# GQA in a Trainium2 decoder kernel: the queries' squares summed by TensorE in fp32, without the split into two bf16 parts

## The chip, the cores and the metric

The kernel runs on one core of one Trainium2 chip. The metric is the device time of one execution in microseconds (us), as the median of several runs.

## The reference, cut to what matters

A two-layer decoder on 64 sequences of 64 tokens with 256 features. Its first block is a grouped-query attention: 16 query heads and 4 key heads of 128 features, each head normalised by its own mean and variance (the layer norm of the queries is the part that the change touches), rotary embedding, causal softmax, output projection. Five more blocks follow (a cross attention, a feed-forward with low-rank experts, a multi-query attention, a second cross attention, a quantised feed-forward), which the change leaves alone.

```python
    def _layernorm(x, g, b):
        mu = jnp.mean(x, axis=-1, keepdims=True)
        var = jnp.mean(jnp.square(x - mu), axis=-1, keepdims=True)
        return (x - mu) * jax.lax.rsqrt(var + EPS) * g + b
    ...
    qkv = jnp.einsum('bsh,oh->bso', x, w_qkv)
    ...
    q = _layernorm(q, qn_g, qn_b)
    k = _layernorm(k, kn_g, kn_b)
    ...
    scores = jnp.einsum('bhqd,bhkd->bhqk', q, k) / jnp.sqrt(jnp.float32(D))
```

## The kernel before

The tokens are 32 tiles of 128 (two sequences each), kept in SBUF for the whole program. Each block of the decoder is a stage of its own that runs over the 32 tiles; the stages follow one another. Within a stage every engine has its own program, in order, and semaphores join them. `over_tiles` writes out the first two and the last two tiles and loops over the rest, two tiles per turn.

In the GQA stage (`attention_gqa`, with the helpers of the class `Attend`) the work of two or three neighbouring tiles is interleaved by hand: in the step of tile t, each engine does the scores and the softmax of t, the projections, squares and rotation of the queries and keys of t + 1, and the values and the output projection of t - 1. The weights are centred per head beforehand, so a head's variance is the mean of the squares of its projected features. Features lie along the partitions and (head, token) along the columns, so a sum over features is a matmul with ones.

The queries of a tile are made in four groups of four heads, one PSUM bank each (`queries`, L103 to L105 through `mm3`). For each group g:

- ScalarE squares the bank into `sq` in fp32 (L596), squares it again into `sqh` in bf16 (L597), and copies the two halves of the features swapped into `qsw` (L600).
- GpSimd multiplies `qsw` by a table into `w` (`swapped_part`, L540), then takes `sql = sq - sqh` as bf16 (`squares_low`, L545).
- VectorE multiplies the bank by another table into `u` (`rotate_query`, L679) and adds `w` (`add_swapped`, L684).

TensorE's order in a step is: transposes of the probabilities of t - 1 (L387), transposes of the normalised x (L274), the scores' bias (L803), the scores (L822), the query sums (`query_sums`, L811 and L812), keys (`mm3` with `a_wk`), values, key sums (L774, fp32, one matmul per key head with `m.ones[:, 0:1]` moving), the first group of queries, the turned scores (L829), values by probabilities (L408), and then the three other groups of queries and the output projection in two halves. The scores wait for all four `add_swapped` (`uw_ready`) and for ScalarE's copy of the transposed probabilities (L393, `pt_ready`), because both use PSUM banks 4 and 5.

On VectorE, the query sums are taken out by L710 into `vq`; GpSimd raises it to the power -1/2 into `rq` (L558); VectorE scales the turned scores by it (L716), adds bias and mask (L720), takes the low part of the first half of the attention output (`ol`, L427; its high part `oh` is ScalarE's L422), the maximum (L355), and so on; L443 adds the output projection to x. GpSimd also subtracts the maximum (L359), scales the probabilities (L379), and takes the layer norm's power (L254, L256) for which VectorE's L266 waits.

Of the kernel before, what the change touches and what calls it, by code (L numbers as in the profile page):

```python
# [20 lines left out]
BF16 = mybir.dt.bfloat16  # L21
ACT = mybir.ActivationFunctionType
AX = mybir.AxisListType.X

P = 128
TILES = 32
SEQ = 64
# [20 lines left out]
def wait_used(eng, sem, t, buffers, per_tile=1, last=0):  # L48

    if isinstance(t, int) and t < buffers:
        return
    eng.wait_ge(sem, (t - buffers) * per_tile + (last or per_tile))
# [158 lines left out]
def spread(a, n):  # L212

    return a.rearrange("p (k o) -> p k o", o=1).to_broadcast([a.shape[0], a.shape[1], n])

def repeat(a, n):

    return a.rearrange("p (o k) -> p o k", o=1).to_broadcast([a.shape[0], n, a.shape[1]])
# [78 lines left out]
HEADS, HD = 16, 128  # L298
# [152 lines left out]
def attention_gqa(m):  # L451
# [9 lines left out]
    with ExitStack() as ctx:  # L461
        sb = lambda n, s, t=F32: ctx.enter_context(nc.sbuf_tensor("a0_" + n, s, t))
        sem = ctx.enter_context(Semaphores(nc, "a0_"))
        ps = ctx.enter_context(nc.psum_tensor("a0_ps", [P, 8, 512], F32))
# [17 lines left out]
        w = sb("w", [P, 2, HEADS, SEQ])  # L482
        qsw = sb("qsw", [P, 2, HEADS, SEQ])
        sq = sb("sq", [P, 2, HEADS, SEQ])
        sqh = sb("sqh", [P, 2, HEADS, SEQ], BF16)
        sql = sb("sql", [P, 2, HEADS, SEQ], BF16)
        st = sb("st", [P, HEADS, SEQ])
        sqk = sb("sqk", [P, NK])
        kt = sb("kt", [P, NK])
# [9 lines left out]
        chain, pool_chain = sem("chain"), sem("pool_chain")  # L499
        k_ready, vp_ready, q_ready, ksum_ready = (sem(n) for n in ("k_ready", "vp_ready", "q_ready", "ksum_ready"))  # L500
        ksw_ready, qsw_ready, u_ready, w_ready = (sem(n) for n in ("ksw_ready", "qsw_ready", "u_ready", "w_ready"))
        sqh_ready, sql_ready, stp_ready, st_ready = sem("sqh_ready"), sem("sql_ready"), sem("stp_ready"), sem("st_ready")
        sqk_ready, sq_ready, uw_ready = sem("sqk_ready"), sem("sq_ready"), sem("uw_ready")
        kraw_ready, vk_ready, rkd_ready, rkb_ready, kt_ready = (sem(n) for n in ("kraw_ready", "vk_ready", "rkd_ready", "rkb_ready", "kt_ready"))
        s2_ready, var_ready, vq_ready, rq_ready = sem("s2_ready"), sem("var_ready"), sem("vq_ready"), sem("rq_ready")
        at_.v_ready = sem("v_ready")
        further = lambda t: not (isinstance(t, int) and t + 2 >= TILES)
        QBANK = (2, 1, 0, 3)
        s2_ps = ps[:, 6, :]
        sct = at_.sc  # L510
        var_ps = ps[:, 7, 0:HEADS]
        heads_of = lambda a: a.rearrange("p (h b s) -> p h b s", h=4, b=2)
        pair_of = lambda a, k, b: a[:, b, 2 * k:2 * k + 2, :].rearrange("p h s -> p (h s)")
        by_head = lambda a, g: a[:, :, 4 * g:4 * g + 4, :].rearrange("p b h s -> p h b s")
# [12 lines left out]
        @block.gpsimd  # L527
        def _(pool):
            def key_rstd(t):
                pool.wait_ge(vk_ready, t + 1)  # L530
                pool.tensor_tensor(rk[:, :], vk[:, :], m.mhalf[:, 0:KV], ALU.pow).then_inc(pool_chain, 1)
                pool.wait_ge(pool_chain, t + 1)
                wait_used(pool, rkb_ready, t, 1)
                pool.tensor_tensor(rkd[:, :, :], repeat(m.ident[:, :], KV), spread(rk[:, :], P), ALU.mult).then_inc(rkd_ready, 1)

            def swapped_part(t, g):

                pool.wait_ge(qsw_ready, 4 * t + g + 1)
                wait_used(pool, uw_ready, t, 1, 4, g + 1)
                pool.tensor_tensor(by_head(w, g), by_head(qsw, g), table(QW), ALU.mult).then_inc(w_ready, 1)  # L540

            def squares_low(t, g):
                pool.wait_ge(sqh_ready, 4 * t + g + 1)
                wait_used(pool, var_ready, t, 1)
                pool.tensor_tensor(by_head(sql, g), by_head(sq, g), by_head(sqh, g), ALU.subtract).then_inc(sql_ready, 1)  # L545

            def head():
                ln.pool(pool)
                ln.pool_step(pool, 1, 1)
                key_rstd(0)  # L550
                pool.wait_ge(tab_set, 1)
                for g in range(4):
                    swapped_part(0, g)
                    squares_low(0, g)

            def step(t, p, has_next):
                pool.wait_ge(vq_ready, t + 1)
                pool.tensor_tensor(rq[:, :], vq[:, :], m.mhalf[:, 0:HEADS], ALU.pow).then_inc(rq_ready, 1)  # L558
                if has_next:
                    key_rstd(t + 1)  # L560
                    swapped_part(t + 1, 0)
                    squares_low(t + 1, 0)
                at_.subtract_max(pool, t)
                if has_next:
                    swapped_part(t + 1, 1)
                    squares_low(t + 1, 1)
                at_.normalise(pool, t)
                if further(t):
                    ln.pool_step(pool, t + 2, p)
                if has_next:  # L570
                    for g in (2, 3):
                        swapped_part(t + 1, g)
                        squares_low(t + 1, g)
            over_tiles(pool, head, step)

        @block.scalar
        def _(act):
            def square_keys(t):
                act.wait_ge(k_ready, t + 1)
                wait_used(act, ksum_ready, t, 1)  # L580
                act.activation(sqk[:, :], ps[:, 1, :], ACT.Square).then_inc(sqk_ready, 1)
                wait_used(act, kraw_ready, t, 1)
                for to, of in swapped:
                    last = act.copy(ksw[to, :], ps[of, 1, :])
                last.then_inc(ksw_ready, 1)

            def value(t, p):
                act.wait_ge(vp_ready, t + 1)
                wait_used(act, at_.pv_ready, t, 2, 2)
                act.activation(at_.v[:, p, :], ps[:, 3, :], ACT.Copy, scale=1.0 / WS).then_inc(at_.v_ready, 1)  # L590

            def square(t, g):
                act.wait_ge(q_ready, 4 * t + g + 1)
                wait_used(act, var_ready, t, 1)
                wait_used(act, sql_ready, t, 1, 4, g + 1)
                act.activation(by_head(sq, g), heads_of(ps[:, QBANK[g], :]), ACT.Square).then_inc(sq_ready, 1)  # L596
                act.activation(by_head(sqh, g), heads_of(ps[:, QBANK[g], :]), ACT.Square).then_inc(sqh_ready, 1)  # L597
                wait_used(act, w_ready, t, 1, 4, g + 1)
                for to, of in swapped:
                    last = act.copy(by_head(qsw[to], g), heads_of(ps[of, QBANK[g], :]))  # L600
                last.then_inc(qsw_ready, 1)

            def scores_out(t):
                act.wait_ge(stp_ready, t + 1)
                wait_used(act, at_.sc_ready, t, 1)
                act.copy(st[:, :, :], sct).then_inc(st_ready, 1)

            def head():
                ln.high(act, 0, 0, q_ready, 4)
                square_keys(0)  # L610
                value(0, 0)
                for g in range(4):
                    square(0, g)

            def step(t, p, has_next):
                before = not (isinstance(t, int) and t == 0)
                if before:
                    at_.copy_transposed(act, t - 1)
                if has_next:
                    ln.high(act, t + 1, 1 - p, q_ready, 4)  # L620
                scores_out(t)
                if has_next:
                    square_keys(t + 1)
                    square(t + 1, 0)
                if before:
                    at_.high(act, t - 1, 0)
                if has_next:
                    square(t + 1, 1)
                at_.exponential(act, t)
                if has_next:  # L630
                    value(t + 1, 1 - p)
                if before:
                    at_.high(act, t - 1, 1)
                if has_next:
                    square(t + 1, 2)
                    square(t + 1, 3)
            over_tiles(act, head, step)
            at_.copy_transposed(act, TILES - 1)
            at_.high(act, TILES - 1, 0)
            at_.high(act, TILES - 1, 1)  # L640
# [111 lines left out]
        def _(pe):  # L752
# [51 lines left out]

            def query_sums(t):

                pe.wait_ge(sql_ready, 4 * (t + 1))
                for b in range(2):
                    for k in range(PAIRS):
                        out = var_ps[:, 2 * k + b:2 * k + b + 1]  # L810
                        pe.matmul(out, pair_of(sqh, k, b), m.onesb[:, :], start=True, stop=False)  # L811
                        last = pe.matmul(out, pair_of(sql, k, b), m.onesb[:, :], start=False, stop=True)  # L812
                last.then_inc(var_ready, 1)

            def scores(t):
# [58 lines left out]
            t, p = TILES - 1, 1  # L874
# [1761 lines left out]
```

## Time and profile before

| | |
|---|---|
| median of 3 runs | 3523.93 us (3517.58 to 3548.65) |
| profiled execution | 3515.81 us, with a span of 3514.0 us from the first to the last instruction |
| mean granted TensorE clock | 0.886 of 2.4 GHz |
| busy: TensorE, VectorE, GpSimd, ScalarE | 2828.3, 2080.2, 1604.8, 1574.2 us |
| scores of the first and of the last GQA tile start at | 86.7 us and 971.6 us |

A profile row gives a start (or a count), a duration, the engine, the line of the kernel, the tensors and their shapes; in brackets stands how long the engine had been idle before it and which instruction released it. PE is TensorE's matmul, DVE is VectorE, ACT is ScalarE, POOL is GpSimd. A matmul's recorded duration includes its way through the array, so neighbouring matmuls overlap in the records; how long a group occupies the engine is read from the start of its first record to the start of the next group. A fp32 matmul shows as two records.

### The profile page before, as it was taken

Reading aid. Unit: us, or ns where it says so; the run is one execution under the profiler, and the core shown is the slowest. Engines: PE = TensorE matmul, PEld = TensorE weight load, DVE = VectorE, ACT = ScalarE, POOL = GpSimd, SP = SyncE. Lnnn points to the kernel's source line nnn. Section 1 sums busy time; section 2 is a strip of 40 time slices with the busy share of each in tenths; the row PEclk is TensorE's granted clock in tenths of the full one; section 3 lists DMA queues with packets and bytes.
Section 4 is the critical chain, followed back from the end, with each engine's and each line's share of the span. In section 5 each row is a group of like instructions: output and inputs, shape, how many; then the busy total and the mean of one; then the engine's idle time right before and its main releaser. Section 6 shows DMA issues by size and latency. Waiting matters only on the chain. (4 is left out here: it accounts for less than half of the span.)

```text
span 3514.0 us, 84894 instructions
## 1 busy us (share of the span) xinstructions
PE 2828.3 (80%) x32044; PEld 2042.3 (58%) x32044; DVE 2080.2 (59%) x3785; ACT 1574.2 (45%) x2718; POOL 1604.8 (46%) x1643
## 2 busy tenths in 40 slices
PE   1788888888857887776699996999999999995665
PEld 1666666666622222223477775878878878884332
DVE  4677777777747667756566663444444444443786
ACT  2555555555516556661233332333333333331665
POOL 1777777777722222213222213545545545541332
PEclk9899999999967557788888888999999999997666
DMA  3000000000012222210000000000000000000000
GB/s 110 1 0 0 0 0 0 0 0 0 0 45 74 69 70 73 79 47 9 19 21 24 21 21 11 7 6 7 7 5 7 7 5 7 7 2 26 12 18 18
DMA packets 94065, 73.24 MB, mean 21 GB/s; under 512 B 17314, under 2 KB 88354, under 8 KB 93218
## 3 DMA queue, kind: packets, MB, share of 16 engines
q1 hardware_dynamic: 93860, 70.14, 6.6%
q8 instruction: 174, 2.85, 0.3%
q14 instruction: 31, 0.25, 0.0%
HBM read 51.76 MB, written 17.04 MB: 20 GB/s over the span
## 5 line engine op out<-in xcount | busy, mean ns | idle before, releaser
L1294 DVE TENSOR_REDUCE x_mx<-x_ps 128x2 f16<-128x512 f32 x512 | 329.8, 682 | 102.1 <-PE x_ps L1356 99.2
L1263 ACT ACTIVATE x_e<-x_ps 128x512 f32<-128x512 f32 x512 | 285.0, 595 | 73.5 <-PE x_ps L1360 67.8
L1356 PE MATMUL x_ps<-x_k,x_q 32*128 32x256 f16 x1024 | 199.1, 336 | 128.2 <-ACT x_e L1263 56.5
L1628 ACT ACTIVATE x_sq<-x_ps 128x512 f32<-128x512 f32 x256 | 152.1, 595 | 310.0 <-PE x_ps L1767 303.2
L1356 PEld LDWEIGHTS x_ps<-x_k,x_q 32*128 32x128 f16 x1024 | 52.9, 97 | 291.2 <-DVE x_mx L1294 153.6
L540 POOL TENSOR_TENSOR a_w<-a_qsw,a_tab 128x512 f32<-128x512 f32 x128 | 218.4, 1706 | 7.9 <-ACT a_qsw L600 6.6
L103 PE MATMUL x_ps<-x_chi,x_w 128*128 128x128 f16 x1024 | 200.3, 221 | 14.3 <-ACT x_rkb L1649 7.5
L1360 PE MATMUL x_ps<-x_q,x_k 32*128 32x256 f16 x1024 | 200.1, 338 | 3.0 <-ACT x_e L1263 2.8
L103 PE MATMUL x_ps<-ln_xhx,x_w 128*128 128x128 f16 x1024 | 198.2, 219 | 1.7 <-DVE x_k L1687 1.7
L104 PE MATMUL x_ps<-x_clo,x_w 128*128 128x128 f16 x1024 | 199.5, 220 | 0.0
L105 PE MATMUL x_ps<-x_chi,x_w 128*128 128x128 f16 x1024 | 199.4, 220 | 0.0
L104 PE MATMUL x_ps<-ln_xlx,x_w 128*128 128x128 f16 x1024 | 197.9, 219 | 0.0
L105 PE MATMUL x_ps<-ln_xhx,x_w 128*128 128x128 f16 x1024 | 197.9, 219 | 0.0
L103 PE MATMUL a_ps<-a_wo,a0oh 128*128 128x256 f16 x512 | 142.8, 279 | 66.2 <-DVE a0ol L427 66.2
L1393 PE MATMUL x_ps<-x_e,x_vt 128*9 128x256 f32 x2048 | 192.4, 510 | 0.9 <-ACT x_e L1263 0.9
L1576 POOL TENSOR_TENSOR x_sum<-x_sum,x_sq 128x512 f32<-128x512 f32 x128 | 162.4, 1268 | 63.1 <-ACT x_sq L1628 57.7
L359 POOL TENSOR_TENSOR x1s<-x1s,x1mx 128x1024 f32<-128x1024 f32 x32 | 60.8, 1901 | 283.1 <-DVE x1mx L355 283.1
L103 PE MATMUL a_ps<-ln_xha,a_wq 128*128 128x128 f16 x1024 | 179.9, 221 | 8.7 <-DVE a_kt L673 8.7
L427 DVE TENSOR_TENSOR x1ol<-x_ps,x1oh 128x1024 f16<-128x1024 f32 x64 | 78.4, 1225 | 180.6 <-ACT x1oh L422 180.6
L104 PE MATMUL a_ps<-ln_xla,a_wq 128*128 128x128 f16 x1024 | 179.3, 221 | 0.0
L105 PE MATMUL a_ps<-ln_xha,a_wq 128*128 128x128 f16 x1024 | 179.3, 221 | 0.0
L545 POOL TENSOR_TENSOR a_sql<-a_sq,a_sqh 128x512 bf16<-128x512 f32 x128 | 164.1, 1282 | 0.0
(343 smaller groups left out, 9699.8 us busy)
## 6 DMA issues: line engine op xcount, KB each, us to landing
x_q<-x_q_rows SPq DMA_DIRECT2D x32, 256.0 KB, 2.7
x_k<-x_k_rows SPq DMA_DIRECT2D x32, 256.0 KB, 3.1
a_stage<-in_x_w SPq DMA_DIRECT2D x32, 256.0 KB, 2.6
x_vt<-in_ctx_v SPq DMA_DIRECT2D x32, 144.0 KB, 2.3
x_all<-in_x SPq DMA_DIRECT2D x8, 512.0 KB, 7.8
x_cf<-in_ctx SPq DMA_DIRECT2D x32, 128.0 KB, 2.1
x_q_rows<-x_xhl SPq DMA_DIRECT2D x32, 128.0 KB, 1.8
x_k_rows<-x_chl SPq DMA_DIRECT2D x32, 128.0 KB, 1.8
```

The source lines that it names most:

```text
L103: pe.matmul(out, a[0], b[0], start=start, stop=False)
L104: pe.matmul(out, a[0], b[1], start=False, stop=False)
L105: return pe.matmul(out, a[1], b[0], start=False, stop=stop)
L540: pool.tensor_tensor(by_head(w, g), by_head(qsw, g), table(QW), ALU.mult).then_inc(w_ready, 1)
L545: pool.tensor_tensor(by_head(sql, g), by_head(sq, g), by_head(sqh, g), ALU.subtract).then_inc(sql_ready, 1)
L1263: act.activation(e[:, u % ES].rearrange("p c n -> p (c n)"), s2_ps(u), ACT.Exp, scale=XT ** -0.5).then_inc(e_ready, 1)
L1294: dve.reduce_max(mx[:, p % 2, c:c + 2], s1_ps(u), AX).then_inc(mx_ready, 1)
L1356: return pe.matmul(s1_ps(u)[:, c], q[r, p % 4, g, c * P:(c + 1) * P], k[r, p % 4, g], start=True, stop=True)
L1360: return pe.matmul(s2_ps(u)[:, c * DM:(c + 1) * DM], k[r, p % 4, g, c * P:(c + 1) * P], q[r, p % 4, g], start=True, stop=True)
L1393: last = pe.matmul(o_ps[32 * jj:32 * jj + VC, g % 2, :], vt[:, p % 2, n, u, :], e[:, u % ES, n, :], start=n == 0, stop=n == KC - 1)
L1576: pool.tensor_tensor(sum4[:, :], sq[:, 0, :] if g == 1 else sum4[:, :], sq[:, g, :], ALU.add).then_inc(sum4_ready, 1)
L1628: act.activation(sq[:, e % 4, :], ps[:, bank(e), :], ACT.Square).then_inc(act_left, 1)
```

## The change

ScalarE no longer writes `sqh`, and GpSimd no longer writes `sql`; both tensors and their semaphores are gone. TensorE sums `sq` directly in fp32, with the 128 columns of a pair of heads as weights and a column of ones moving: 16 matmuls per tile with fp32 operands in the place of 32 with bf16 operands. It waits for `sq_ready` in the place of `sql_ready`.

```diff
@@ gpsimd
-            def squares_low(t, g):
-                pool.wait_ge(sqh_ready, 4 * t + g + 1)
-                wait_used(pool, var_ready, t, 1)
-                pool.tensor_tensor(by_head(sql, g), by_head(sq, g), by_head(sqh, g), ALU.subtract).then_inc(sql_ready, 1)
...
-                    squares_low(0, g)
...
-                    squares_low(t + 1, 0)
...
-                    squares_low(t + 1, 1)
...
-                        squares_low(t + 1, g)
@@ scalar, square(t, g)
-                wait_used(act, sql_ready, t, 1, 4, g + 1)
                 act.activation(by_head(sq, g), heads_of(ps[:, QBANK[g], :]), ACT.Square).then_inc(sq_ready, 1)
-                act.activation(by_head(sqh, g), heads_of(ps[:, QBANK[g], :]), ACT.Square).then_inc(sqh_ready, 1)
@@ tensor, query_sums(t)
-                pe.wait_ge(sql_ready, 4 * (t + 1))
+                pe.wait_ge(sq_ready, 4 * (t + 1))
                 for b in range(2):
                     for k in range(PAIRS):
-                        out = var_ps[:, 2 * k + b:2 * k + b + 1]
-                        pe.matmul(out, pair_of(sqh, k, b), m.onesb[:, :], start=True, stop=False)
-                        last = pe.matmul(out, pair_of(sql, k, b), m.onesb[:, :], start=False, stop=True)
+                        last = pe.matmul(var_ps[:, 2 * k + b:2 * k + b + 1], pair_of(sq, k, b), m.ones[:, 0:1], start=True, stop=True)
```

## Rows read from the trace of the kernel before

**Rows 1.** The page: busy time by engine, and the group of L545.

```profile
PE 2828.3 (80%) x32044; PEld 2042.3 (58%) x32044; DVE 2080.2 (59%) x3785; ACT 1574.2 (45%) x2718; POOL 1604.8 (46%) x1643
...
L545 POOL TENSOR_TENSOR a_sql<-a_sq,a_sqh 128x512 bf16<-128x512 f32 x128 | 164.1, 1282 | 0.0
```

**Rows 2.** Windows: length, busy PE, PEld, DVE, ACT, POOL, granted clock, DMA.

```profile
400.00:500.00 100.00, 82.55 (x946) 64.12 (x943) 70.70 (x100) 54.86 (x87) 76.11 (x52) 1.00 0.00 0
```

**Rows 3.** Timeline of VectorE: L716 of the third and the 31st tile.

```profile
158.93 1.23 DVE L716 TENSOR_TENSOR a0s<-a_ps,a_rq 128x1024 f32<-128x1024 f32 x1 [0.54 <-PE a_ps L829]
...
952.90 1.23 DVE L716 TENSOR_TENSOR a0s<-a_ps,a_rq 128x1024 f32<-128x1024 f32 x1 [0.54 <-PE a_ps L829]
```

**Rows 4.** Waits in the GQA stage: us in total, times, longest.

```profile
DVE a_u L684 <- POOL a_w L540: 38.3, 31, 1.2
```

**Rows 5.** Timeline of VectorE in one tile.

```profile
501.86 1.22 DVE L427 TENSOR_TENSOR a0ol<-a_ps,a0oh 128x1024 f16<-128x1024 f32 x1
...
513.20 1.35 DVE L266 TENSOR_SCALAR ln_xna<-x_all,ln_mva,ln_rstda 128x256 f32 x1 [0.45 <-POOL ln_rstda L256]
...
515.07 0.41 DVE L443 SCALAR_TENSOR_TENSOR x_all<-a_ps,x_all 128x256 f32 x1
515.40 0.71 DVE L684 TENSOR_TENSOR a_u<-a_u,a_w 128x512 f32<-128x512 f32 x1
517.34 1.56 DVE L684 TENSOR_TENSOR a_u<-a_u,a_w 128x512 f32<-128x512 f32 x1 [1.23 <-POOL a_w L540]
...
527.57 1.23 DVE L716 TENSOR_TENSOR a0s<-a_ps,a_rq 128x1024 f32<-128x1024 f32 x1 [0.54 <-PE a_ps L829]
```

**Rows 6.** Timeline of GpSimd in the same tile.

```profile
512.06 1.11 POOL L256 TENSOR_TENSOR ln_rstda<-ln_vea,mhalf 128x1 f32<-128x1 f32 x1
513.14 1.26 POOL L540 TENSOR_TENSOR a_w<-a_qsw,a_tab 128x512 f32<-128x512 f32 x1
514.36 1.20 POOL L545 TENSOR_TENSOR a_sql<-a_sq,a_sqh 128x512 bf16<-128x512 f32 x1
515.52 1.72 POOL L540 TENSOR_TENSOR a_w<-a_qsw,a_tab 128x512 f32<-128x512 f32 x1
517.19 1.16 POOL L545 TENSOR_TENSOR a_sql<-a_sq,a_sqh 128x512 bf16<-128x512 f32 x1
522.15 2.90 POOL L558 TENSOR_TENSOR a_rq<-a_vq,mhalf 128x16 f32<-128x16 f32 x1 [3.80 <-DVE a_vq L710]
```

**Rows 7.** Timeline of ScalarE in the same tile.

```profile
500.65 1.01 ACT L422 CAST a0oh<-a_ps 128x1024 f16<-128x1024 f32 x1
...
502.22 0.59 ACT L597 ACTIVATE a_sqh<-a_ps 128x512 bf16<-128x512 f32 x1
...
516.73 1.01 ACT L393 COPY a0pt<-a_ps 128x1024 f32<-128x1024 f32 x1 [3.57 <-PE a_ps L387]
```

**Rows 8.** Timeline of TensorE in the same tile.

```profile
515.63 1.06 PE L387 MATMUL a_ps<-ident,a0e 128*128 128x128 f32 x8 [1.85 <-DVE x_all L443]
...
516.75 1.02 PE L803 MATMUL a_ps<-a_kt,a_bq 128*128 128x512 f32 x2
518.95 1.95 PE L822 MATMUL a_ps<-a_u,a_kt 128*64 128x256 f32 x16 [1.18 <-DVE a_u L684]
520.83 0.18 PE L811 MATMUL a_ps<-onesb,a_sqh 128*128 128x1 bf16 x1
...
521.65 0.22 PE L103 MATMUL a_ps<-ln_xha,a_wk 128*128 128x128 f16 x1
...
524.28 0.95 PE L774 MATMUL a_ps<-ones,a_sqk 128*128 128x1 f32 x8
525.09 0.22 PE L103 MATMUL a_ps<-ln_xha,a_wq 128*128 128x128 f16 x1
```

**Rows 9.** Timelines of VectorE and TensorE before the first scores.

```profile
82.57 4.05 DVE L684 TENSOR_TENSOR a_u<-a_u,a_w 128x512 f32<-128x512 f32 x4
...
86.67 3.68 PE L822 MATMUL a_ps<-a_u,a_kt 128*64 128x256 f32 x16 [4.96 <-DVE a_u L684]
```

More of the change, by code:

```diff
@@ L484, in attention_gqa @@
         sq = sb("sq", [P, 2, HEADS, SEQ])
-        sqh = sb("sqh", [P, 2, HEADS, SEQ], BF16)
-        sql = sb("sql", [P, 2, HEADS, SEQ], BF16)
         st = sb("st", [P, HEADS, SEQ])
@@ L501, in attention_gqa @@
         ksw_ready, qsw_ready, u_ready, w_ready = (sem(n) for n in ("ksw_ready", "qsw_ready", "u_ready", "w_ready"))
-        sqh_ready, sql_ready, stp_ready, st_ready = sem("sqh_ready"), sem("sql_ready"), sem("stp_ready"), sem("st_ready")
+        stp_ready, st_ready = sem("stp_ready"), sem("st_ready")
         sqk_ready, sq_ready, uw_ready = sem("sqk_ready"), sem("sq_ready"), sem("uw_ready")
```

## The prediction

> **What bounds the kernel now.** The page comes first [rows 1]: the change touches only the first attention (GQA, to about 1,004 us), and TensorE is the busiest engine of the whole. The page's chain that ended last is no help: it covers only the final instructions of the last stage. So the stage is read on its own. In a stretch of 100 us there TensorE shows 82.6 us busy, GpSimd 76.1, VectorE 70.7, ScalarE 54.9, at a granted clock of 1.00, the 2.4 GHz level [rows 2]. No engine is full: the tile is bound by a loop that passes through several of them. L716, the scaling of the scores, starts once per tile, and its first and last regular starts, 158.93 and 952.90, are 28 tiles apart: 28.36 us per tile [rows 3], with the same wait each time. One tile can therefore stand for all.
>
> I follow the loop backwards from L716 at 527.57. It waits for TensorE (0.54 us, the turned scores) [rows 5]. TensorE has had no gap since the scores' matmuls at 518.95: scores, query sums, keys, values, key sums, first queries, turned scores all follow in program order [rows 8]. The scores waited for the last addition of the rotated queries, L684, that ends at 517.34 + 1.56 = 518.90 [rows 5]. This in turn waited for GpSimd's product L540, which ends at 515.52 + 1.72 = 517.24 [rows 6]; the list of waits has this one in 31 tiles, 38.3 us in all [rows 4]. Ahead of it VectorE is in one nearly unbroken row from L716 to the residual L443, which ends at 515.48 and lets TensorE start its transposes at 515.63 [rows 5, 8]. So a tile is: VectorE's long stretch, then the join of L684 with GpSimd's L540, then TensorE's unbroken stretch of 8.6 us from the scores to the next L716.
>
> **TensorE's part: on the path.** Old: 32 matmuls with bf16 weights of 128 columns and one moving column occupy TensorE from 520.83 to 521.65, 0.82 us [rows 8]. New: 16 with fp32 weights. The kernel already has this very form, in the key sums L774: four matmuls, which the trace shows as eight records, from 524.28 to the next operation at 525.09, so 0.81 us, or 0.20 per matmul [rows 8]. Sixteen make 3.24 us, so the step grows by 2.42 us. The first load hides under the matmul ahead in both places. A run of 32 records need not go exactly like one of eight, and the key sums' end is read off the next operation's start. Bounds for the 16: 3.0 and 3.5 us, growth 2.2 to 2.7.
>
> The row first: a fp32 load-and-multiply record follows the last one after 0.10 us, a bf16 one after 0.026 [rows 8]. The Trainium skill (TensorE: Matmul & The Clock Gate, "Weight-path perf modes" and "LDWEIGHTS") says that the fast weight load is off for fp32 weights and that an ordinary load takes the number of columns over 1.2 ns, 107 ns for 128 columns. This rule speaks against the change; an estimate by that page is 32 times 0.107, or 3.41 us, 0.17 us a tile or 5 us in all more than by the row.
>
> Behind these matmuls on TensorE's queue wait the keys, the values, the key sums, the first queries and the turned scores, and L716 waits for the last of them. There is no wait in this stretch that could absorb the 2.42. GpSimd's power L558 (for the queries' factors) shifts by as much: it begins at 522.15 and ends at 525.06, 2.5 us ahead of L716 [rows 5, 6], and as both shift alike it stays ahead.
>
> **GpSimd's part: L545 goes.** Four subtractions per tile, 1.28 us each in the mean [rows 1], 5.1 us. Most of this buys nothing. Behind L540 of groups 0 and 1 GpSimd waits for VectorE's maximum or denominator anyway, and those two L545 are in that idle time. What counts is the L545 of group 2, between the two last products [rows 6], and that of group 3. The rows show GpSimd and VectorE taking turns: L684 with both inputs in SBUF takes 0.68 to 0.71 alone, but the last one takes 1.56 and ends 0.55 after GpSimd's L545 (517.19 + 1.16 = 518.35; 518.90). L540 takes 1.26 alone and 1.72 where L684 runs before it [rows 5, 6]. The Trainium skill (SBUF — State Buffer, on the shared port pair) calls this an exclusive lock, held for the whole instruction, against GpSimd for VectorE's operations with two SBUF inputs; this trace agrees.
>
> New order, in the times of the old tile, with 0.12 us taken off throughout: the cast L422 at 500.65 waits for ScalarE's copies, which come one L597 (0.59) earlier; its product is wanted at 501.86, and L427 can start only when VectorE's preceding addition ends, which I put at 501.74 [rows 5, 7]. The power L256, L540 of group 2 (513.02 to 514.28) and L266 (to 514.43) keep their order. L540 of group 3 comes next, and with the port free from 514.43 takes 1.13: to 515.56. L684 of group 2 waits for it and ends 0.55 later, 516.11. L684 of group 3 follows directly, with nothing of GpSimd's in the way, and ends at about 516.8. The join moves from 518.90 to 516.8: 2.1 us.
>
> **What is late next.** TensorE cannot use all of it. Its transposes L387 wait for L443 (now 515.36), so they start at 515.51; the bias matmul L803 starts at 516.63 and its records end at 517.65. And the scores overwrite the banks that L393, ScalarE's copy of the transposed probabilities, reads: L393 begins when L387 is through and ends at 516.73 + 1.01 - 0.12 = 517.62 [rows 7, 8]. Scores then start at 517.68 and not at 518.95: 1.27 us gained per tile. Bounds: 0.9, if L803's queue or the semaphores take 0.35 more; 1.6, if the 0.12 turns out as 0.4.
>
> **ScalarE's part: L597 goes.** Four of 0.59 us [rows 7]. ScalarE waits for TensorE before the squares and idles after the last copies, so this is worth only the 0.12 above. No DMA, and no queue of SP's, is touched. The wait of the sums is now on ScalarE's square and not on GpSimd's remainder; both are long done at 520.8, so this is worth nothing; if that cover were gone it would cost the distance from the square to the sums.
>
> **The sum.** Per regular tile 2.42 - 1.27 = +1.15 us. All 32 tiles pay the 2.42: +77.4. Tiles 1 to 31 take back 1.27: -39.4. The start: before the first scores ScalarE does four L597, two of them ahead of the keys for which the third group of queries waits, and GpSimd's L545 stretch the four additions L684 to 4.05 us [rows 9] instead of four steps of 0.6 plus one wait; I work out 2.1 us earlier for ScalarE's last copy and 1.0 for the additions, -3.1. In tile 1 the limit by L393 is absent (its probabilities are early), so about 1.4 more comes back there. The two first score blocks run at a clock near 1.2 GHz (3.68 us against 1.95 [rows 8, 9]); the fp32 sums behind them would be dearer by up to 3 us each, and some of that comes back because the clock rises in the same stretch while later work benefits: +1 net, bounds -2 to +5. Together 77.4 - 39.4 - 3.1 - 1.4 + 1 = +34.5 us.
>
> The profiled execution took 3515.8 us around a span of 3514.0; with the sum it would be 3550. The runs of before have a median of 3523.9, lowest 3517.6: the profile is at their lower end, 8 us under the median. Against the median I forecast 3558. About 1% is what a measurement of this kernel can tell from no change, and the sum is 0.98% of the median: whether it is called slower or the same is nearly a toss.
>
> **The rivals.**
> (1) No recovery. Another wait takes the place of L540's, and the scores start no earlier. For it: VectorE's rows are dense, and L803 and L393 are only 1.2 us behind. Against it: both rows show their ends, and neither waits for the removed work. All of the 2.42 is then paid: 77.4 - 3.1, so +74, 3598 us.
> (2) Cheaper sums. Long runs of fp32 loads with one column pipeline better than four; the sixteen take 2.4 us (0.075 per record). For it: the four L774 stand between other forms. Against it: eight equal records are already a run. The growth is 1.6, the tile +0.3, the total about 32 x 0.82 = 26 less: +8, 3532 us.
> (3) The port turns the other way: this is the faster case. L256 and L684 of group 1 come to the port within 0.05 us, L256 takes 1.11 and loses about 0.55; L266 comes 0.06 after L540 of group 2 and takes 1.35, some 0.9 of it waiting [rows 5, 6]. The 0.12 shift, or GpSimd's emptier queue, could let L256 and L266 go first. Then L443, TensorE's transposes and the scores are up to 1.45 us earlier, the tile goes to 2.42 - 1.27 - 1.45 = -0.30, and the total to -10: 3514 us. It turns to a gain from 1.15 us on. Against it: all four operations hang on the same denominator and shift together, so that the order should stay. That alone is under 1%; with cheaper sums, or a larger gain before the scores, it would pass 1%.
>
> **How the numbers follow.** Forecast with its bounds 0.67, rival 1 0.10, rival 2 0.12, rival 3 0.11. The forecast's own bounds: growth less gain from 2.2 - 1.6 = 0.6 to 2.7 - 0.9 = 1.8 us a tile, so +18 to +55 us; against 3517 to 3524 as the base 3535 to 3579. The range reaches over half of rival 2 and part way to rival 1: 3532 to 3585. Slower by over 1%: half of the forecast less a little (its sum is just under 1%), 0.34, and rival 1, 0.10: 0.44. Faster by over 1%: 0.06, the part of rival 3 that comes together with cheaper sums. The same: 0.50, the rest of all of them.
>
> **What the next profile would show.** Right: L716 regularly 29.5 us apart; the sums from the first record to the keys' first matmul 3.2 us; L684 of the last group 0.68 and no longer 1.56; scores waiting for ScalarE's copy L393 or following L803 at once; GpSimd idle 5 us more per tile. Wrong: a distance of 30.8 (rival 1), sums of 2.4 (rival 2), L266 at about 0.45 (rival 3). What would upset all of it is a granted clock other than 1.00 in the regular tiles, where I count on no change because TensorE's share of busy time rises.

## The result and the profile after

The changed kernel takes 3707.9 us (median of 4 runs, 3694.5 to 3720.3) against 3521.9 for the kernel before (median of 4 runs now): 1.051 times as long, with an interval of 1.047 to 1.055. The forecast was 3558 us with 3585 as its upper end. The kernel is slower by 186 us where 35 were forecast.

The page after, busy times and granted clock:

```profile
PE 3038.8 (82%) x32044; PEld 2220.8 (60%) x32044; DVE 2081.2 (56%) x3785; ACT 1512.9 (41%) x2590; POOL 1405.2 (38%) x1515
...
PEclk9988898898887578765878887999999999998566
```

GpSimd lost 200 us of work and ScalarE 61, and TensorE gained 210 [rows 1 for before]. As far as the 13th slice, where the first attention ends, the clock's digits are now mostly 8, where the tiles of before ran at 1.00 [rows 2]. The lines have new numbers: L703 is the scaling of the scores (was L716), L707 adds bias and mask (L720), L671 is the addition of the rotated queries (L684), L538 GpSimd's product (L540), L797 the query sums (L811, L812), L807 the scores (L822), L761 the key sums (L774).

VectorE's timeline, with the first and the last regular start of L703 and one tile between:

```profile
160.60 1.23 DVE L703 TENSOR_TENSOR a0s<-a_ps,a_rq 128x1024 f32<-128x1024 f32 x1 [1.54 <-PE a_ps L814]
...
502.22 1.22 DVE L703 TENSOR_TENSOR a0s<-a_ps,a_rq 128x1024 f32<-128x1024 f32 x1 [1.54 <-PE a_ps L814]
503.48 2.12 DVE L707 TENSOR_TENSOR a0s<-a0s,a_s2m 128x1024 f32<-128x1024 f32 x1
505.74 1.23 DVE L427 TENSOR_TENSOR a0ol<-a_ps,a0oh 128x1024 f16<-128x1024 f32 x1
...
518.94 0.41 DVE L443 SCALAR_TENSOR_TENSOR x_all<-a_ps,x_all 128x256 f32 x1
519.27 1.42 DVE L671 TENSOR_TENSOR a_u<-a_u,a_w 128x512 f32<-128x512 f32 x2
...
536.42 1.23 DVE L703 TENSOR_TENSOR a0s<-a_ps,a_rq 128x1024 f32<-128x1024 f32 x1 [1.52 <-PE a_ps L814]
...
1116.64 1.23 DVE L703 TENSOR_TENSOR a0s<-a_ps,a_rq 128x1024 f32<-128x1024 f32 x1 [1.54 <-PE a_ps L814]
```

A tile takes (1116.64 - 160.60) / 28 = 34.14 us, 5.79 more than before [rows 3]. GpSimd's and ScalarE's rows of the same tile:

```profile
501.63 1.04 POOL L532 TENSOR_TENSOR a_rkd<-ident,a_rk 128x512 f32<-128x512 f32 x1
503.24 1.27 POOL L538 TENSOR_TENSOR a_w<-a_qsw,a_tab 128x512 f32<-128x512 f32 x1 [0.57 <-ACT a_qsw L587]
```

```profile
520.59 1.01 ACT L393 COPY a0pt<-a_ps 128x1024 f32<-128x1024 f32 x1 [4.53 <-PE a_ps L387]
```

TensorE's timeline, in two stretches of the same tile:

```profile
521.75 1.95 PE L807 MATMUL a_ps<-a_u,a_kt 128*64 128x256 f32 x16
523.62 4.81 PE L797 MATMUL a_ps<-ones,a_sq 128*128 128x1 f32 x32
528.29 0.27 PE L103 MATMUL a_ps<-ln_xha,a_wk 128*128 128x128 f16 x1
...
530.81 0.63 PE L103 MATMUL a_ps<-a_wv,ln_xha 128*128 128x512 f16 x1
...
533.13 0.95 PE L761 MATMUL a_ps<-ones,a_sqk 128*128 128x1 f32 x8
```

And windows (length, busy PE, PEld, DVE, ACT, POOL, granted clock, DMA) over that stretch:

```profile
522.00:525.00 3.00, 3.00 (x29) 2.40 (x25) 0.93 (x2) 1.01 (x1) 0.00 (x0) 1.00 0.00 0
525.00:526.00 1.00, 1.00 (x12) 1.00 (x11) 0.00 (x0) 0.00 (x0) 0.00 (x0) 1.00 0.00 0
526.00:527.00 1.00, 1.00 (x7) 1.00 (x7) 0.00 (x0) 0.00 (x0) 0.00 (x0) 0.52 0.00 0
527.00:532.00 5.00, 5.00 (x34) 4.26 (x35) 0.17 (x1) 0.92 (x2) 2.90 (x1) 0.50 0.00 0
532.00:533.00 1.00, 1.00 (x4) 0.39 (x3) 0.12 (x1) 0.83 (x2) 0.00 (x0) 0.56 0.00 0
533.00:534.00 1.00, 1.00 (x12) 0.97 (x11) 1.00 (x2) 0.00 (x0) 0.00 (x0) 1.00 0.00 0
```

These are the rows to look at.
The tile of before (499.19 to 527.57, [rows 5, 8]) and this one (502.22 to 536.42), piece by piece along the loop of the prediction. Of the tile of before these rows are wanted as well, from VectorE and GpSimd:

```profile
499.19 1.23 DVE L716 TENSOR_TENSOR a0s<-a_ps,a_rq 128x1024 f32<-128x1024 f32 x1 [0.54 <-PE a_ps L829]
500.45 1.27 DVE L720 TENSOR_TENSOR a0s<-a0s,a_s2m 128x1024 f32<-128x1024 f32 x1
```

```profile
499.60 1.04 POOL L534 TENSOR_TENSOR a_rkd<-ident,a_rk 128x512 f32<-128x512 f32 x1
500.79 2.06 POOL L540 TENSOR_TENSOR a_w<-a_qsw,a_tab 128x512 f32<-128x512 f32 x1
```

| piece, us | before | after | difference |
|---|---|---|---|
| L716/L703 to the end of the residual L443 | 16.29 | 17.13 | +0.84 |
| to the first score matmul | 3.47 | 2.40 | -1.07 |
| scores | 1.88 | 1.87 | 0 |
| query sums, to the first key matmul | 0.82 | 4.67 | +3.85 |
| keys and values, to the key sums | 2.63 | 4.84 | +2.21 |
| to the next L716/L703 | 3.29 | 3.29 | 0 |

The last L703 of the stage starts 165.9 us later than L716 did (1144.1 against 978.2), and that is the change's doing. The other 29 us between the two profiled executions (3710.5 and 3515.8) lie in later stages, whose code is the same. The second stage takes 521 us from its first to its last reduction before and 538 after, but between 494 and 552 in the kernels below, which leave it alone too. I did not look into what moves it; it also widens the intervals, so the tile's length in the trace is the sharper measure here.

### The profile page after: what moved, and what is told of

Read it like the earlier page. It is cut to its first block and busy times, and to the rows that moved or that the text cites. A ratio compares the mean times of both kernels' runs of the same rounds, so it can differ in the third digit from the quotient of the medians.

```text
span 3708.1 us, 84512 instructions
## 1 busy us (share of the span) xinstructions
PE 3038.8 (82%) x32044; PEld 2220.8 (60%) x32044; DVE 2081.2 (56%) x3785; ACT 1512.9 (41%) x2590; POOL 1405.2 (38%) x1515
## 5 line engine op out<-in xcount | busy, mean ns | idle before, releaser
L1378 PE MATMUL x_ps<-x_e,x_vt 128*9 128x256 f32 x2048 | 202.2, 532 | 0.9 <-ACT x_e L1248 0.9
L550 POOL TENSOR_TENSOR a_rq<-a_vq,mhalf 128x16 f32<-128x16 f32 x32 | 93.2, 2911 | 289.4 <-DVE a_vq L697 289.4
L538 POOL TENSOR_TENSOR a_w<-a_qsw,a_tab 128x512 f32<-128x512 f32 x128 | 177.9, 1399 | 21.1 <-ACT a_qsw L587 21.0
```

The costliest lines, as they stand in the source:

```text
L1378: last = pe.matmul(o_ps[32 * jj:32 * jj + VC, g % 2, :], vt[:, p % 2, n, u, :], e[:, u % ES, n, :], start=n == 0, stop=n == KC - 1)
```

## The experiments

The tile's length is the distance of the third from the 31st L716 (or its line in that kernel) over 28. The clock is that of the window from 200 to 800 us.

| run | what | ratio to before (interval) | median us | tile us | clock |
|---|---|---|---|---|---|
| before | | | 3521.9 | 28.36 | 1.00 |
| changed | | 1.051 (1.047 to 1.055) | 3707.9 | 34.14 | 0.90 |
| pe_only | fp32 sums, split kept | 1.048 (1.038 to 1.057) | 3688.9 | 33.51 | 0.93 |
| split_only | split gone, bf16 sums | 0.989 (0.982 to 0.997) | 3482.3 | 27.21 | 1.00 |
| wide_sums | 128 moving columns | 1.017 (1.009 to 1.024) | 3580.8 | 30.13 | 1.00 |
| bf16_long | 4 times the bf16 sums | 1.027 (1.019 to 1.035) | 3617.3 | 31.01 | 0.99 |
| fp16_squares | one fp16 square | 0.985 (0.982 to 0.989) | 3472.9 | 26.88 | 1.00 |
| port_wait | GpSimd waits for L703 | 1.035 (1.030 to 1.039) | 3650.9 | 32.55 | 0.92 |
| halves | 8 sums, keys, 8 sums | 1.022 (1.016 to 1.028) | 3595.9 | 30.85 | 1.00 |
| cols32 | 32 moving columns | 1.038 (1.034 to 1.041) | 3658.7 | 31.93 | 0.95 |
| halves_port | both of these | 1.012 (1.005 to 1.020) | 3579.0 | 30.00 | 1.00 |
| bf16_longer | 8 times the bf16 sums | one run | 3786.6 | 36.32 | 0.89 |

**Each part by itself.** First, which part brings the clock down.

```diff
 # before.py, query_sums; squares and split stay
-                        out = var_ps[:, 2 * k + b:2 * k + b + 1]
-                        pe.matmul(out, pair_of(sqh, k, b), m.onesb[:, :], start=True, stop=False)
-                        last = pe.matmul(out, pair_of(sql, k, b), m.onesb[:, :], start=False, stop=True)
+                        last = pe.matmul(var_ps[:, 2 * k + b:2 * k + b + 1], pair_of(sq, k, b), m.ones[:, 0:1], start=True, stop=True)
```

> TensorE's part alone: 16 fp32 matmuls with one moving column sum sq, while ScalarE's second square and GpSimd's subtraction stay, their results unused. Theory A, thin sums: a few us of matmuls with one moving column let the granted clock fall, in whatever type. Then the sums take about 4.7 us, keys and values run at half clock, and the tile is 28.4 + 3.9 + 2.2 = 34.5 us: about 3715 us. Theory B, fp32 itself: the same. Theory C, the rhythm: the clock falls because the removed work on ScalarE and GpSimd changed the waits of TensorE. Then the clock stays at 1.00 here, the tile is 28.4 + 2.4 = 30.8 us, and the time about 3600 us.

3688.9 us. The clock falls though ScalarE and GpSimd do all that they did before, so the rhythm of their work is not the cause (theory C). In 19 of the 28 tiles the whole price is there (33.9 to 34.4 us), in four part of it (32.8), and five take the 31.1 us of a full clock; why the clock spares these, where it falls in every tile of the changed kernel, stays open. In one of the five the sixteen sums take 3.60 us, from 464.77 to the first key matmul at 468.37. The tile at 575 us, in windows:

```profile
597.00:600.00 3.00, 3.00 (x29) 3.00 (x27) 0.00 (x0) 1.01 (x1) 0.00 (x0) 0.97 0.00 0
600.00:606.00 6.00, 6.00 (x37) 4.62 (x38) 0.34 (x2) 1.76 (x3) 2.90 (x1) 0.50 0.00 0
```

```diff
 # after.py: one square, in bf16; 32 sums of it
-        sq = sb("sq", [P, 2, HEADS, SEQ])
+        sq = sb("sq", [P, 2, HEADS, SEQ], BF16)
...
-                        last = pe.matmul(var_ps[:, 2 * k + b:2 * k + b + 1], pair_of(sq, k, b), m.ones[:, 0:1], start=True, stop=True)
+                        out = var_ps[:, 2 * k + b:2 * k + b + 1]
+                        pe.matmul(out, pair_of(sq, k, b), m.onesb[:, :], start=True, stop=False)
+                        last = pe.matmul(out, pair_of(sq, k, b), m.onesb[:, :], start=False, stop=True)
```

This kernel leaves the low part of the squares out and counts the high part twice, so its results are of no use; it is there for its time.

> The split's removal alone: ScalarE squares once, into bf16, GpSimd does nothing, and TensorE sums the same bf16 squares in 32 matmuls of one column, each tile twice, as many as before and in the same type (the sums are twice the squares' high parts). Theories A and B: clock 1.00 in every regular tile, sums 0.8 us, the scores 1.1 to 1.3 us nearer to the residual's end; tile 27.1 to 27.3 us and 3480 to 3490 us, unless GpSimd's first product takes the port ahead of VectorE's addition of bias and mask (L720), as in the changed kernel: then 0.85 us more per tile and 3510 us. Theory C: the clock falls in each tile here, and the time is above 3550 us.

3482.3 us, tile 27.21. The removal of the split is a gain, of the size expected: the scores start 2.40 us behind the residual's end (3.47 before). In 5 of the 28 tiles it is 26.8 and not 27.3; there the residual ends 0.5 us earlier. In each of them GpSimd's L256 takes 0.55 us and not 1.10, so it had the port ahead of VectorE's L671, which is half of rival 3; single tiles of other kernels do the same. No tile showed the other half, L266 ahead of GpSimd's product: L266 takes 1.3 us or more in all of them.

**Thin, or fp32.**

```diff
 # after.py, query_sums
-                for b in range(2):
-                    for k in range(PAIRS):
-                        last = pe.matmul(var_ps[:, 2 * k + b:2 * k + b + 1], pair_of(sq, k, b), m.ones[:, 0:1], start=True, stop=True)
+                for k in range(PAIRS):
+                    for b in range(2):
+                        i = 2 * k + b
+                        last = pe.matmul(ps[:, 7, i:i + P], pair_of(sq, k, b), m.ones[:, :], start=True, stop=True)
```

> The changed kernel, with 128 moving columns of ones in the place of one, in ascending order, so that each matmul's first column stays and the others are overwritten. The array is busy for nearly the same time (a fp32 record of 128 columns follows the last after 0.11 us, one of a single column after 0.10). Theory A: the clock stays at 1.00, sums 3.6 us, tile 28.4 + 2.8 - 1.1 + (0 to 0.85) = 30.1 to 31 us, 3570 to 3600 us, faster than the changed kernel though TensorE does more. Theory B: the clock falls as in the changed kernel or more, at least 3710 us.

3580.8 us and a tile of 30.13, 4.0 us less than with a single column, although TensorE streams 128 times the columns. Its window over the regular tiles, against that of the changed kernel:

```profile
200.00:800.00 600.00, 526.85 (x5349) 427.89 (x5347) 399.63 (x577) 286.73 (x437) 334.43 (x220) 1.00 0.00 0
```

```profile
200.00:800.00 600.00, 519.69 (x4714) 418.81 (x4712) 369.40 (x514) 253.61 (x386) 278.20 (x194) 0.90 0.00 0
```

The busy shares shown are 88% and 87%, the clocks 1.00 and 0.90: the two kernels cannot be told apart by the busy share. The type alone (theory B) is not the cause either, since the operands are fp32 in both. What differs is the number of moving columns, and the order of the sixteen (k before b); cols32 below has this same order, and there the clock falls, so the order is not what keeps it up.

```diff
 # before.py, query_sums: around both loops, 8 in bf16_longer
+                for _ in range(4):
...
```

> The kernel before with its bf16 sums done four times over: 128 matmuls of one column, about 3.3 us, as long as the fp32 sums should have been. Theory A: the clock falls here too, in about the same place; the sums themselves hardly notice (0.026 to 0.027 us each at either clock), keys and values take 2.2 us more: tile 28.4 + 2.4 + 2.2 = 33 us, about 3670 us. Theory B: the clock stays at 1.00, tile 30.8, about 3600 us.

> The kernel before with its bf16 sums done eight times over, 256 matmuls of one column, about 6.5 us. With four times over the clock fell in a few tiles only. If a thin stretch in bf16 counts as a lull like one in fp32, only less so, then at this length the clock falls in every tile, keys and values take 4.8 instead of 2.6 us, and the tile is 28.36 + 5.6 + 2.2 = 36.2 us, 3760 us. If only fp32 does it, the clock stays at 1.00, the tile is 34.0 us, and the time 3700 us.

Four times over, theory A was wrong as I had put it: the clock stays up in nearly all tiles (30.76 us each; 5 of the 28 took 32.2 to 32.4), the mean tile is 31.01, and not 33. Eight times over it falls in every tile: none of the 28 took the 34.0 us of a full clock, they took 35.4 to 37.6, mean 36.32, where I expected 36.2. So one-column matmuls in bf16 bring the clock down too: 3.2 us of them in few tiles, 6.7 us in every one. Whether bf16 needs a longer stretch than fp32 is not shown, since the fp32 sums take 3.6 us and no bf16 run has that length.

```diff
 # after.py, order k, b and i = 2 * k + b as in wide_sums
...
+                        last = pe.matmul(ps[:, 7, i:i + 32], pair_of(sq, k, b), m.ones[:, 0:32], start=True, stop=True)
```

> The changed kernel with 32 moving columns per fp32 sum instead of 1 or 128. Theory: what counts is how many columns stream per us. The sums should take 3.2 us, as their duration is set by the weight loads; if 32 columns are enough, the clock stays at 1.00 and the tile is 28.36 + 2.42 - 1.07 = 29.7 us, 0.4 less than with 128 columns; about 3565 us. If they are not enough, it falls as with one column: 34 us, about 3700.

Neither: tiles of 30.0 stand beside tiles of 34.2, with a mean of 31.93, and the clock is 0.95. The tiles of 30.0 are the changed kernel's tile at a full clock (the sums take 3.6 us there). What exactly brings the clock down stays open: with 32 columns per 0.11 us it fell in many tiles, and with one bf16 column per 0.026 us, over a slightly shorter stretch, in few.

**The length of the stretch.**

```diff
 # after.py: query_sums(t, b) does the 8 sums of sequence b
...
-                query_sums(t)
+                query_sums(t, 0)
                 if has_next:
                     keys(t + 1, 1 - p)
+                query_sums(t, 1)
+                if has_next:
                     value(t + 1, 1 - p)
```

> The changed kernel with 8 of the 16 fp32 sums ahead of the keys and 8 behind them. TensorE's work is the same, but a thin stretch is half as long. Theory: the length of the stretch brings the clock down; so it stays at 1.00 here, the tile is 28.36 + 2.42 - 1.07 = 29.7 us, and the time 3560 us or so. Rival: only the amount of thin work in a tile counts, however it is laid out; then the clock falls as in the changed kernel, and the time is about 3700 us.

The clock stays at 1.00 with exactly the same 16 thin fp32 matmuls; so it is not their amount per tile but the stretch in one piece. TensorE's timeline:

```profile
525.38 1.95 PE L796 MATMUL a_ps<-ones,a_sq 128*128 128x1 f32 x16
527.18 0.22 PE L103 MATMUL a_ps<-ln_xha,a_wk 128*128 128x128 f16 x1
...
528.52 1.90 PE L796 MATMUL a_ps<-ones,a_sq 128*128 128x1 f32 x16
```

The tile is 30.85 and not 29.7. The rows give both reasons. Eight sums take 1.80 us (525.38 to 527.18), so 16 take 3.6 and not 3.24. And the residual ends 17.12 us behind L703, not 16.3: the order at the port, which is turned here as in the changed kernel.

**The order at the port.**

```diff
 # after.py, GpSimd's step
                     key_rstd(t + 1)
+                    pool.wait_ge(at_.sc_left, t + 1)
                     swapped_part(t + 1, 0)
```

> The changed kernel, with GpSimd's first product of a tile (L538) waiting until VectorE has scaled the scores (L703), so that VectorE's L707 comes to the shared port first, as it did before. If the order at the port costs 0.85 us per tile, L707 goes from 2.1 to 1.27 us, the residual's end comes 16.3 us behind L703 instead of 17.1, and the tile from 34.14 to 33.3: about 26 us less than the changed kernel. If something else sets L427 and what follows, nothing changes. The clock still falls in each tile.

In the tile at 556 us, L707 (here L708) takes 1.23 again and the residual ends 16.24 us behind L703. Tiles with the whole low stretch take 33.3 (34.2 before the wait), as expected. In about every second tile the low stretch is shorter too (31.7 us), so the mean tile is 1.59 us shorter, 45 us over the 28. The run as a whole gained 57 us and not 26; the rest lies outside these tiles.

> The two halves of the sums, and GpSimd's wait of the run before last. If the clock and the order at the port are the only two things that went otherwise than forecast, then with both held off the changed kernel does what the forecast said, but for the sums' price, which the runs with a full clock put at 3.6 us and not 3.24: tile 28.36 + 2.75 - 1.07 = 30.0 us, clock 1.00, L707 1.23 to 1.27 us, the residual's end 16.3 us behind L703; about 53 us more than the kernel before, 3575 us. A third cause would leave it at 30.5 or more.

A tile of 30.00 us, in all 28 (29.98 to 30.02), as expected. GpSimd's and VectorE's rows:

```profile
526.12 1.04 POOL L532 TENSOR_TENSOR a_rkd<-ident,a_rk 128x512 f32<-128x512 f32 x1
527.71 2.14 POOL L538 TENSOR_TENSOR a_w<-a_qsw,a_tab 128x512 f32<-128x512 f32 x1 [0.54 <-DVE a0s L704]
```

```profile
526.23 1.22 DVE L704 TENSOR_TENSOR a0s<-a_ps,a_rq 128x1024 f32<-128x1024 f32 x1 [1.54 <-PE a_ps L815]
527.49 1.23 DVE L708 TENSOR_TENSOR a0s<-a0s,a_s2m 128x1024 f32<-128x1024 f32 x1
```

VectorE's L708 starts 0.22 us ahead of GpSimd's L538, and now it is L538 that is stretched. With clock and order both held off, the tile is what the forecast's terms give with the sums at their measured price: nothing else is left to explain in it. The median is 3579, where the forecast was 3558 and this run's own expectation 3575.

**A version that beats both.**

```diff
 # after.py
-        sq = sb("sq", [P, 2, HEADS, SEQ])
+        sq = sb("sq", [P, 2, HEADS, SEQ], F16)
...
-                act.activation(by_head(sq, g), heads_of(ps[:, QBANK[g], :]), ACT.Square).then_inc(sq_ready, 1)
+                act.activation(by_head(sq, g), heads_of(ps[:, QBANK[g], :]), ACT.Square, scale=1.0 / WS).then_inc(sq_ready, 1)
...
-                dve.tensor_scalar(vq[:, :], var_ps, 1.0, HD * LN_EPS * WS * WS, ALU.mult, ALU.add).then_inc(vq_ready, 1)
+                dve.tensor_scalar(vq[:, :], var_ps, WS * WS, HD * LN_EPS * WS * WS, ALU.mult, ALU.add).then_inc(vq_ready, 1)
...
-                        last = pe.matmul(var_ps[:, 2 * k + b:2 * k + b + 1], pair_of(sq, k, b), m.ones[:, 0:1], start=True, stop=True)
+                        last = pe.matmul(var_ps[:, 2 * k + b:2 * k + b + 1], pair_of(sq, k, b), m.onesh[:, 0:1], start=True, stop=True)
```

> ScalarE writes each square once, divided by 64 squared so that it fits, in fp16; TensorE sums it in 16 matmuls of one column with fp16 weights, and VectorE's L697 multiplies by 64 squared again. No split, no fp32 matmul. Theory thin and slow sums (a long stretch of one-column fp32 matmuls brings the clock down): the sums take 16 times 0.026, 0.4 us, clock 1.00, the scores 2.4 us behind the residual's end instead of 3.5; tile 28.36 - 0.41 - 1.07 = 26.9 us, 46 us less than the kernel before, about 3475 us. Theory C, the rhythm: the clock falls in this kernel as well.

3472.9 us, 0.985 of before (0.982 to 0.989), tile 26.88. The sums:

```profile
489.22 1.95 PE L807 MATMUL a_ps<-a_u,a_kt 128*64 128x256 f32 x16
491.10 0.55 PE L797 MATMUL a_ps<-onesh,a_sq 128*128 128x1 f16 x16
```

It keeps the change's gain (-1.07) and turns its price into a second gain (-0.41). The squares are rounded once, to fp16, where the changed kernel keeps them in fp32.

## Why the prediction was wrong

**The step that failed** is the last sentence on the profile to come: "a granted clock other than 1.00 in the regular tiles, where I count on no change because TensorE's share of busy time rises". The share did rise, and the clock fell. Its direct price is the difference between the changed kernel and halves, which does the same work at a full clock and with the order at the port turned as well: 34.14 - 30.85, or 3.30 us a tile from the unrounded lengths, over half of the 5.79. About 1.1 us of it is in the sums themselves (4.67 against 3.6) and 2.2 in the keys and values behind them, which the change does not touch. The rows of before showed that the clock can be low in this stage (the first scores, [rows 9]), but held no long stretch of one-column matmuls; I priced those by their duration alone and put the clock at nothing. The Trainium skill (TensorE: Matmul & The Clock Gate, "Why this matters for your kernels") names idle gaps between bursts of matmuls as what throws the clock back. The trace differs: the records of the changed kernel show no gap there. Measurement decides: in this kernel the clock fell in a stretch that the profile shows as fully busy.

**The price of the sums** was mis-sized: 3.24 forecast, 3.6 measured at a full clock (1.80 for eight). I divided the 0.81 us of L774 by eight records. But from the start of its first matmul to the next operation there are only seven full intervals between fp32 loads, as the first load lies under the matmul ahead; and 0.81 / 7 = 0.116 times 31 gives 3.59. That is an estimate after the fact; halves has 0.112 a record (1.80 over 16), where I had 0.10. This was 0.33 us a tile, just beyond the bound of 3.5.

**The order at the port** is rival 3's mechanism with the sign turned: I had a shift of 0.12 us forwards and considered that it might help. It came at another place, L720/L707 against the first product of the tile. In the tile of before VectorE's L720 starts first (500.45), takes 1.27, and GpSimd's L540 is stretched to 2.06; in the changed kernel L538 starts 0.24 us ahead of L707 (503.24 against 503.48), takes 1.27, and L707 is stretched to 2.12. Two things had to come together for this, and I had neither: I put the removal of L597 at the 0.12 us alone, and no change of the clock.

One is the missing L597: without it the product's input from ScalarE is ready 0.86 us behind L703, where it was 1.43 behind L716. It is needed: pe_only keeps L597, and there L720 takes no more than 1.27 in any tile, low clock or not. And it is not enough: in wide_sums, at a full clock, GpSimd is still busy with its key factors L532 until VectorE has the port, in all 28 tiles. GpSimd's and VectorE's rows:

```profile
459.24 1.04 POOL L532 TENSOR_TENSOR a_rkd<-ident,a_rk 128x512 f32<-128x512 f32 x1
460.24 2.25 POOL L538 TENSOR_TENSOR a_w<-a_qsw,a_tab 128x512 f32<-128x512 f32 x1
```

```profile
458.83 1.23 DVE L703 TENSOR_TENSOR a0s<-a_ps,a_rq 128x1024 f32<-128x1024 f32 x1 [0.54 <-PE a_ps L815]
460.09 1.27 DVE L707 TENSOR_TENSOR a0s<-a0s,a_s2m 128x1024 f32<-128x1024 f32 x1
```

Its sums are as long as in the changed kernel at a full clock (3.67 us), so the longer sums do not turn the order either. The other thing is an early start of L532: 0.59 us ahead of L703 in the changed kernel, 0.41 behind it in wide_sums and in before. L532 follows from the keys, and between the keys and L703 TensorE does the values. At the low clock these take longer (530.81 to 533.13, 2.32 us, where before took 1.29), so L703 comes later behind the keys, and GpSimd is free before VectorE is. The turned order is thus a consequence of the low clock. Within one kernel, cols32 shows it: the tile at 387 follows a full clock, the one at 420 a low stretch.

```profile
387.99 1.27 DVE L707 TENSOR_TENSOR a0s<-a0s,a_s2m 128x1024 f32<-128x1024 f32 x1
...
421.38 2.11 DVE L707 TENSOR_TENSOR a0s<-a0s,a_s2m 128x1024 f32<-128x1024 f32 x1
```

In halves it is the second eight sums that lie between the keys and L703, so there the order turns at a full clock. The turned order costs 30.85 - 30.00 = 0.85 us a tile, by halves against halves_port.

**The recovery** was right in mechanism: L671 of the last group runs directly behind its neighbour (1.42 us for both, where the last alone took 1.56 and had waited 1.23), the scores follow ScalarE's L393 (520.59 + 1.01 = 521.60, scores at 521.75), and rival 1 did not come true. Its size was 1.07 against 1.27, of which 0.12 was the shift that did not come and 0.08 a start of the scores later behind the residual than I put it (2.40 us, not 2.32).

In sum per tile: forecast +1.15; +0.33 for the sums, +0.16 for the recovery and the shift as halves_port has them, which makes 30.00 - 28.36 = 1.64; +3.30 for the low clock directly and +0.85 for the port, which the low clock turned: 5.79. So 4.15 of the 5.79 hang on the clock. The tiles of cols32 agree: 30.0 to 30.1 us with a full clock in the tile and ahead of it, 34.1 to 34.2 with a low stretch in both. Over the 28 regular tiles this is 162 of the 165.9 us; the rest is at the ends. The bounds of the range came from durations and waits only, and had nothing for the clock.

## What to carry to other kernels

A matmul with one moving column can cost more than its time. In this kernel 3.6 us of them in fp32 dropped TensorE to half its clock, and the work behind paid, directly and by the order at the port that VectorE and GpSimd share. Keep such stretches short (two of 1.8 us did no harm here), lay other matmuls between them, give them more moving columns where that is free (128 here), or use a 16-bit type (the sixteen took 0.41 us in fp16), before counting on "TensorE is busy". And where an edit or a slower neighbour makes a GpSimd operation ready earlier against VectorE's, look at which VectorE operation it can now overtake at the shared port; earlier is not always better.

## What the runs showed that I had not expected

- The clock fell to the 1.2 GHz level with TensorE shown busy without a gap, about halfway through 4.7 us of one-column fp32 matmuls, and came back some 4.6 us after denser work (the keys) had begun. The same matmuls in two groups of 1.8 us, with 1.3 us of keys between, never did this in the window from 200 to 800 us.
- With 128 moving columns in the place of one, 16 fp32 matmuls took hardly longer (3.67 against 3.6 us) and kept the clock at 1.00; 32 columns kept it only in part (0.95).
- 128 one-column bf16 matmuls (3.2 us) let it fall in a few tiles, 256 (6.7 us in the tile looked at) in every one.
- The winner of a 0.2 us race at the port is worth 0.85 us a tile; one wait on a semaphore that was there already settles it.
- In the changed kernel that race was lost because of the low clock: with the same work on GpSimd, ScalarE and VectorE at a full clock (tiles of cols32, all of wide_sums) VectorE came first.
